# A vision transformer layer on one core: q and k transposed without gap columns and spread by DMA, token tables joined in DRAM, order of work remade

## The reference

```
h = patches @ W_lin.T + b_lin                 # 64 x 196 x 192
h = [cls_tok, cls_token, h]                   # 198 tokens an image
q, k, v = split(layernorm(h) @ w_qkv.T)       # 12 heads of 16
q, k = rope(q * 0.25), rope(k)                # rotation by the token's place
h = h + softmax(q @ k.T) @ v @ w_proj.T + b_proj
h = h + ffn(layernorm(h))
```

## Time and profile before

| | us |
|---|---|
| median of three executions | 1359.68 |
| the profiled execution | 1361.1 |
| its span | 1359.3 |
| TensorE busy (share) | 1312.5 (97%) |
| VectorE | 981.5 (72%) |
| ACT | 901.0 (66%) |
| POOL | 890.1 (65%) |
| mean granted clock of TensorE | 0.974 |

### The profile page before, as it was taken

How to read it: one execution, slowest core, us unless ns; L and a number is a source line. 1 busy time by engine, 2 the same in 40 slices (tenths; PEclk the granted TensorE clock), 3 DMA queues, 4 the chain that set the end, 5 groups by cost and what they waited for, 6 DMA issues and landing times.

```text
span 1359.3 us, 38194 instructions
## 1 busy us (share of the span) xinstructions
PE 1312.5 (97%) x13142; PEld 989.3 (73%) x13142; DVE 981.5 (72%) x2318; ACT 901.0 (66%) x1629; POOL 890.1 (65%) x1610
## 2 busy tenths in 40 slices
PE   6689999999999999999999999999999999999888
PEld 5467777777777777777777777777777777777667
DVE  1346777877777787777787777787777778776665
ACT  1235677677777777777767767767777777776564
POOL 5445676776667777677676676677666777766243
PEclk9779999999999999999999999999999999999799
DMA  5412212222212222222212222222221222200000
GB/s 151 108 39 58 57 45 55 73 67 62 64 48 76 57 68 58 62 57 55 75 56 54 63 66 59 53 72 67 63 62 48 75 57 68 55 24 20 4 20 27
DMA packets 141809, 79.64 MB, mean 59 GB/s; under 512 B 52631, under 2 KB 140918, under 8 KB 141526
## 3 DMA queue, kind: packets, MB, share of 16 engines
q1 hardware_dynamic: 140428, 74.42, 21.1%
q10 hardware_dynamic: 1194, 2.79, 0.8%
HBM read 56.48 MB, written 9.73 MB: 49 GB/s over the span
## 4 chain that ended last, share of the span: by engine, by line
PE 92%; SPq 2%; DVE 2%; ACT 1%; issue 1%; DMA 1%; POOL 1%; POOLq 0%; ACTq 0%; DVEq 0%
PE turn L463 15%; PE score L525 12%; PE turn L481 11%; PE turn L547 10%; PE turn L592 7%; PE score L504 5%; PE turn L534 5%; PE turn L491 4%; PE turn L600 4%; PE turn L573 4%; PE turn L556 3%; PE turn L574 2%; PE turn L610 2%; PE turn L445 2%; PE turn L581 2%; PE turn L566 2%
## 5 line engine op out<-in xcount | busy, mean ns | idle before, releaser
L885 DVE TENSOR_REDUCE nmax<-score 99x8 f32<-99x1584 f32 x192 | 347.0, 1808 | 130.7 <-PE score L504 130.7
L704 ACT ACTIVATE prob<-score 99x1584 f32<-99x1584 f32 x192 | 286.5, 1492 | 88.1 <-PE score L525 88.1
L463 PE MATMUL turn<-wlin,xp 128*128 128x192 f32 x1188 | 228.1, 343 | 7.0 <-DMA xp<-in_x 7.0
L463 PEld LDWEIGHTS turn<-wlin,xp 128*128 128x128 f32 x1188 | 198.5, 196 | 18.5 <-POOL onT L1009 5.1
L1034 POOL TENSOR_TENSOR ropec<-qk,rope 128x384 f32<-128x384 f32 x99 | 99.0, 1000 | 161.0 <-ACT qk L680 161.0
L525 PE MATMUL score<-qkT 17*99 17x198 f32 x3072 | 182.1, 352 | 18.3 <-DMA qkT<-nmaxT 11.0
L525 PEld LDWEIGHTS score<-qkT 17*99 17x99 f32 x3072 | 117.8, 163 | 76.6 <-issue 65.2
L481 PE MATMUL turn<-wqkv,xT 96*128 96x384 f32 x396 | 156.2, 518 | 1.9 <-ACT xT L673 1.8
L547 PE MATMUL turn<-prob,vaug 99*32 99x198 f32 x3072 | 151.9, 337 | 0.0
L1064 POOL TENSOR_TENSOR yg<-y,gout 128x512 f32<-128x512 f32 x99 | 125.6, 1268 | 29.8 <-ACT yr L765 18.4
L934 DVE SCALAR_TENSOR_TENSOR ag<-th,turn 128x512 f32<-128x512 f32 x99 | 68.0, 687 | 75.9 <-ACT th L744 75.9
(11 more groups left out here) (97 smaller groups left out, 2663.3 us busy)
## 6 DMA issues: line engine op xcount, KB each, us to landing
xp<-in_x SPq DMA_DIRECT2D x63, 588.0 KB, 4.7
out<-h SPq DMA_DIRECT2D x99, 96.0 KB, 1.9
qkT<-nmaxT SPq DMA_DIRECT2D x192, 3.1 KB
vaug<-vt SPq DMA_DIRECT2D x30, 78.9 KB
bias<-in_added SPq DMA_DIRECT2D x30, 74.2 KB
win<-in_win ACTq DMA_DIRECT2D x1, 768.0 KB
xp<-in_x SPq DMA_DIRECT2D x2, 294.0 KB, 5.4
wlin<-in_wlin ACTq DMA_DIRECT2D x2, 288.0 KB, 4.1
```

Of the source, the lines that this page charges most:

```text
L463: last = pe.matmul(turn[:, k, 0:D], xp[:, c, place:place + TILE], wlin[:, c, :], start=(c == 0), stop=(c == KC - 1))
L704: act.activation(prob[:, :, 4 * g:4 * g + 4, :].rearrange("p t r n -> p r t n"), score[0:TT, :, 0:2 * TOKENS].rearrange("p r (t n) -> p r ...
L885: dve.tensor_reduce(nmax[:, b % 2, :, 4 * g:4 * g + 4].rearrange("p t r -> p r t"), score[0:TT, :, 0:2 * TOKENS].rearrange("p r (t n) -> p ...
```

## The change

It has three parts.

1. *q and k.* `qkp` has no gaps, so `transpose_qk` makes three transposes of 128 columns instead of six and takes one bank. A column of a transposed chunk is then 128 head dimensions, eight heads. ACT copies them to a new buffer `qkd`, and SyncE (`place_qk`) puts them to every second row of `qkT` with two DMAs a tile (four where the ring wraps). The heads' rows between were set once, 0 for q and 1 for k, by VectorE. The maxima go to row 31 of each head; the score matmuls take 32 rows, those for the maxima 31. `round_qkT` waits for the DMAs instead of ACT.
2. *Tables.* ACT issues six DMAs at the start which join the three tables, twice one after the other, in a scratch array in DRAM; from tile 1 on, one DMA of 128 rows x 224 columns loads a tile's tables, six tiles deep. Tile 0 comes from the three arrays by six DMAs.
3. *Order.* Attention of an image starts two steps later than before (max scores at half step 2 x tile + 10 instead of + 6), `PROJ_AT` with it; there are 118 steps, and the store comes a step earlier after the projection. Each engine's loop body lists the stages in another order.

```diff
-            top.append(max(top[-1] + 1 if top else 0, 2 * (final_tile(b) + 2) + 2))
-        turn.append(top[-1])
+            top.append(max(top[-1] + 1 if top else 0, 2 * (final_tile(b) + 3) + 4))
+        turn.append(top[-1] + 1)
         for g in range(GROUPS):
-            soft.append(max(soft[-1] + 1 if soft else 0, turn[-1] + 2))
-        out.append(soft[-1] + 2)
+            soft.append(max(soft[-1] + 1 if soft else 0, turn[-1] + 1))
+        out.append(soft[-1] + 3)
...
-        steps.append(max(steps[-1] + 1 if steps else 0, (OUT_AT[final_image(i)] + 2) // 2))
+        steps.append(max(steps[-1] + 1 if steps else 0, (OUT_AT[final_image(i)] + 1) // 2))
...
-STEPS = PROJ_AT[-1] + 9
+STEPS = PROJ_AT[-1] + 8
...
+    tab_d = nc.dram_tensor("joined", (2 * TOKENS, TAB), F32, kind="Internal").ap()
...
-        qkp = sb("qkp", [128, 2, 2 * HEADS, 2 * DH])
+        qkp = sb("qkp", [128, 2, QK])
+        qkd = sb("qkd", [128, 2, GROUPS, TILE])
...
+            def load_tab(i):
+                if i >= TABS:
+                    sp.wait_ge(rope_done, i - TABS + 1)
+                at = TILE * i % TOKENS
+                sp.dma_start(tab[:, i % TABS, :], tab_d[at:at + TILE, :]).then_inc(tab_loaded[i % TABS], 16)
...
+            def place_qk(i):
+                if i == 0:
+                    sp.wait_ge(qkT_cleared, 2)
+                sp.wait_ge(qkT_copied, i + 1)
+                over = (TILE * (i + 1) - 1 - QRING) // TOKENS
+                if over >= 0:
+                    sp.wait_ge(st_ready, 3 * over + 3)
+                for place, lo, n in pieces(TILE * i, TILE, QRING):
+                    for half in range(2):
+                        sp.dma_start(qkT[0:128:2, half:2 * GROUPS:2, place:place + n],
+                                     qkd[64 * half:64 * half + 64, i % 2, :, lo:lo + n]).then_inc(qk_placed[i % 2], 16)
...
+            load_tab_parts(0)
             load(1)
-            load_bias(0)
+            sp.wait_ge(tables_joined, 16 * 6)
+            for i in range(1, FIRST_TABS):
+                load_tab(i)
             load(2)
...
-            for s in range(-3, STEPS):
-                for i in tile_at(s + 1):
-                    next_rope(i)
+            for s in range(-2, STEPS):
+                for i in tile_at(s - 6):
+                    place_v(i)
                 for b in at(NMAX_AT, 2 * s):
                     place_max(b)
-                for i in tile_at(s - 2):
-                    place_v(i)
+                for i in tile_at(s - 4):
+                    place_qk(i)
+                for i in at(PROJ_AT, s - 7):
+                    store(i)
+                for i in tile_at(s + 2):
+                    prepare(i)
                 for b in at(NMAX_AT, 2 * s + 1):
                     place_max(b)
...
-                k = take(("qkT", i), 2, qkT_copied, Q_COPIES[i])
-                for side in range(2):
-                    for g in range(GROUPS):
-                        head = side * HEADS + 4 * g
-                        last = pe.transpose(turn[:, k + side, g * TILE:(g + 1) * TILE],
-                                            qkp[:, i % 2, head:head + 4, :].rearrange("p h d -> p (h d)"),
-                                            ident[:, :])
+                k = take(("qkT", i), 1, qkT_copied, i + 1)
+                for c in range(GROUPS):
+                    last = pe.transpose(turn[:, k, c * TILE:(c + 1) * TILE], qkp[:, i % 2, c * 128:(c + 1) * 128],
+                                        ident[:, :])
...
-                        rows = slice(32 * r, 32 * r + DH)
+                        rows = slice(32 * r, 32 * r + 31)
...
-                        rows = slice(32 * r, 32 * r + DH + 1)
+                        rows = slice(32 * r, 32 * r + 32)
...
+            for copy in range(2):
+                rows = tab_d[copy * TOKENS:(copy + 1) * TOKENS, :].rearrange("(h a) c -> a h c", h=2)
+                act.dma_start(rows[:, :, 0:D], bias_d[:, :, :]).then_inc(tables_joined, 16)
+                act.dma_start(rows[:, :, D:D + DH], cos_d[:, :, D:D + DH]).then_inc(tables_joined, 16)
+                act.dma_start(rows[:, :, D + DH:TAB], sin_d[:, :, D:D + DH]).then_inc(tables_joined, 16)
...
             def round_qkT(i):
-                pool.wait_ge(qkT_copied, Q_COPIES[i])
+                pool.wait_ge(qk_placed[i % 2], qk_count(i))
```

More of the change, by code:

```diff
@@ L111, in token_runs, with qk_count @@
     return runs
+def qk_count(i):
+    return sum(32 * len(pieces(TILE * n, TILE, QRING)) for n in range(i % 2, i + 1, 2))
 def beyond(i):
@@ L243, in build @@
         begun_embed = sem("begun_embed")
-        bias_loaded = [sem(f"bias_loaded{p}") for p in range(BBUF)]
-        rope_loaded = [sem(f"rope_loaded{p}") for p in range(TBUF)]
+        tables_joined = sem("tables_joined")
+        tab_loaded = [sem(f"tab_loaded{p}") for p in range(TABS)]
         stored = [sem(f"stored{p}") for p in range(TBUF)]
@@ L258, in build @@
         rope_done = sem("rope_done")
+        qkT_cleared = sem("qkT_cleared")
         qkT_ready = sem("qkT_ready")
         qkT_copied = sem("qkT_copied")
+        qk_placed = [sem(f"qk_placed{p}") for p in range(2)]
         qkT_rounded = sem("qkT_rounded")
@@ L344, in prepare @@
                         load(b + XSLOT)
[L346 to L351, removed]
-                            .then_inc(rope_loaded[i % TBUF], 16)
             def place_v(i):
@@ L620, in _ @@
                     max_scores(n)
+                for b in at(NMAX_AT, 2 * s):
+                    transpose_max(b)
+                for b in at(OUT_AT, 2 * s - 1):
+                    transpose_on(b)
+                for b in at(OUT_AT, 2 * s - 2):
+                    transpose_on(b)
                 for i in tile_at(s):
@@ L683, in copy_qkT @@
                 act.wait_ge(qkT_ready, i + 1)
-                over = (TILE * (i + 1) - 1 - QRING) // TOKENS
-                if over >= 0:
-                    act.wait_ge(st_ready, 3 * over + 3)
-                k = bank_of["qkT", i]
-                src = turn[:, k:k + 2, 0:GROUPS * TILE].rearrange("p a (g n) -> p a g n", g=GROUPS)
-                for place, lo, n in pieces(TILE * i, TILE, QRING):
-                    act.activation(qkT[:, :, place:place + n].rearrange("p (a g) n -> p a g n", a=2),
-                                   src[:, :, :, lo:lo + n], ACT.Copy).then_inc(qkT_copied, 1)
+                if i >= 2:
+                    act.wait_ge(qk_placed[i % 2], qk_count(i - 2))
+                act.activation(qkd[:, i % 2, :, :], turn[:, bank_of["qkT", i], 0:QK].rearrange("p (g n) -> p g n", g=GROUPS),
+                               ACT.Copy).then_inc(qkT_copied, 1)
             def copy_maxT(b):
@@ L961, in _ @@
             dve.memset(ones[:, :], 1.0).then_inc(setup_dve, 1)
-            for s in range(-3, STEPS):
+            dve.memset(qkT[:, 0:GROUPS, :], 0.0).then_inc(qkT_cleared, 1)
+            dve.memset(qkT[:, GROUPS:2 * GROUPS, :], 1.0).then_inc(qkT_cleared, 1)
+            for s in range(-2, STEPS):
                 if s == SUM_STEP:
@@ L1078, in norm_y @@
                 pool.tensor_tensor(kap3[:, c], vpow[:, c], kap[:, c], ALU.mult).then_inc(norm3, 1)
-            for s in range(-3, STEPS):
-                for i in at(PROJ_AT, s - 2):
-                    norm_y(i)
+            for s in range(-2, STEPS):
                 for i in at(PROJ_AT, s):
```

176 lines of the change are left out of this document (78 added, 98 removed).

## The result

The changed kernel takes 1315.21 us (median of four runs, 1313.17 to 1318.29), against 1359.30 us for the kernel before measured beside it: a ratio of 0.968, 95% interval 0.966 to 0.970. The forecast was 1319 us in 1300 to 1348.

| stretch of the span, us | before | predicted | after |
|---|---|---|---|
| start to step 14 | 162.0 (163.4 in the sum) | 125.5 | 127.3 |
| 85 steps, 14 to 98 | 1074.4 | 1044.7 | 1038.6 |
| one of them | 12.64 | 12.29 | 12.22 |
| step 99 to the end | 122.9 | 148.6 | 145.4 |

A forecast was written before the change was run, and what follows sets the result against it. TensorE's own work, 97% busy, was taken to bound the kernel. Start 125.5 + 85 steps x 12.29 (1044.7) + end 148.6 = 1318.8 us of span, plus 0.4: 1319 us, range 1300 to 1348.

The forecast's parts named there:

- The added lag: End of the kernel: two more attention steps at 13.9 us each add 27.8 us.
- A full step: Middle, TensorE: three transposes fewer at 0.109 us each save 0.33 us of 12.62, 28 us over 85 steps.
- sign of a misread transpose: Middle: a step shrinking by other than 0.3 us with TensorE full would mean the transpose's price was misread.
- four borders before and four after: TensorE's changes into score groups: about 0.1 us each, four per step before and after, so left out.
- TensorE stays fed: Middle, score banks: new legs of 2.72 to over 3 us exceed floors of 2.63 and 2.44, the tightest by 0.11.
- Rival 1: Middle: the score loop swallows the saving; legs 0.3 us longer per step lose the 28 us, giving 1347 us; 12%.
- The placing: SyncE's transfers of q and k between ACT's copy and POOL's rounding: 2.3 us to landing after issuing, hidden.
- The start: Up to step 14: 125.5 us against 163.4, with the 11.0 us stall and half the clock's loss gone.
- Step 6: Start: this step begins at 36 to 42 us, taken as 39.5, after six steps of embedding and projections.
- rival 3: Start stays as it is: the stall came from the weights' and x's loads and meets the placings; 1337 us; 12%.
- The eight steps after it: Start, steps 6 to 13: 104.4 us before less 18.3 makes 86 us, bounds 79 to 93.
- The clock: Start: 14.6 us of full clock lost after the stall, half of it (7.3) regained; added score rows cost nothing.

The follow-up runs named there:

- experiment 7: Changed kernel with score matmuls over 17 and 16 rows instead of 32 and 31, leaving out head dimensions and the maximum's row: 1323.80 us.
- 1: Changed kernel with each tile's three transposes of q and k made twice: 1343.86 us.
- 2: Kernel before with only the joined tables and one table load per tile, old order, lag and six transposes: 1349.47 us.
- 9: Kernel before with score matmuls over 32 rows instead of 17 and 16, the added rows of q being zeros: 1346.58 us.
- 3: Changed kernel's q and k transposes, spreading by DMA and joined tables, but in the order and with the lag of the kernel before: 1355.03 us.
- 5: Kernel of 3 with the FFN's output product moved behind the attention's projection, and its addition on VectorE behind the residual: 1336.69 us.
- Experiment 4: Changed kernel with FFN weights loaded in four parts over four steps instead of at once, and summed two steps later: 1306.76 us.
- 6: Kernel of 5 with the FFN weights loaded in four parts over steps 2 to 5: 1333.53 us.
- 10: Changed kernel with 17 rows in the exponential's score matmuls alone, leaving out the maximum's row too: 1323.98 us.
- 11: Changed kernel with 16 rows in the maxima's score matmuls alone: 1315.61 us.

## Why the prediction was right, and where it was not

The time lies 4 us under the forecast, and in part by luck: without the rows' effect on the clock, which the prediction did not know, it would by experiment 7 be some 1324 us, 5 us over. The parts of the change do not add up one by one, since they meet at the start, but three are measured alone: the transposes 28.7 us (1), the tables 8.8 (2), the rows 8.6 to 11.3 (7, 9). The added lag costs its two steps at the end.

- *A full step, 12.29 predicted, 12.22 measured.* Three transposes were priced at 0.33 us, and giving them back costs 0.307. The step before is 12.64 over the 85 steps counted (12.62 was the mean of 87), so it shrank by 0.42 and not by 0.33: the prediction's sign of a misread transpose, without one. The sum held that four borders before and four after cancel. They do in number, but not in size: xr's 0.37 us became 0.22, 0.15 less, and qkp's new border takes only 0.1 back; the embedding gives 0.07. That xr's 0.37 held a wait at the loop's floor besides the border, as the prediction allowed, fits this; no run separates the two.
- *TensorE stays fed.* Right: the score loop has legs of 2.91 and 2.68 us and no wait in the middle. But the argument stood on the new order, and I had not seen how much: with the old one the saving is swallowed (3), by a leg that rows 3 showed at 2.64 us. Rival 1 was given 12% by the margin of the new legs; the row that spoke "against it" (a leg at its floor cost nothing) was really the reason why the saving needed another order. One group moved into that leg recovers 0.30 us a step (5).
- *The placing.* Landing 2.4 us for 2.3, SyncE's two issues 0.66 us each for the allowed 0.5: hidden in the middle, as worked out. The 2.2 us that the Trainium skill ("DMA: Bandwidth & Descriptors", Anatomy of one DMA) gave is a fit for transfers that GpSimd issues; these are SyncE's, and the 2.4 measured decides. That the placing's lateness is what the longer lag is for, the theory of 3, is not borne out: with the old lag TensorE waited 2.1 us in all for the round.
- *The start, 125.5 predicted, 127.3 measured*, came out by two errors of opposite sign. Step 6 was taken at 39.5 us and begins at 44.85, since the weights' load does meet the placings: rival 3 in part, with another victim (POOL's round) and 6.7 us instead of 11. Experiment 4 shows the remedy for this one. The Trainium skill ("DMA: Bandwidth & Descriptors", Why a DMA increments its semaphore by 16 and not by 1) had been held against that rival, because the cuts of the old tables go to few engines; experiment 2 agrees that the tables were at fault (1.6 us instead of 11.0), though not that it was through the number of engines. But that section says nothing of a wide transfer that lands behind 768 KB, and of these the slowest landed 8.4 us after its issue. The eight steps after it then took 127.3 - 44.85 = 82.4 us, for 86.
- *The clock* was the misread term. "More rows take no longer, and I cost the added ones at nothing": the first half holds, the second does not. They hold up the granted clock where TensorE's work has gaps, which is worth 8.6 us in the changed kernel (7) and 11.3 in the one before (9). The loss before was put down to the stall alone, and half of it credited to the stall's end. From 61 to 104 us the clock was 0.66 before, 0.77 with the stall gone and few rows (2), 0.80 in the new order with few rows (7), and 0.88 with all. The end profited too: the whole stretch from step 99 ran at 0.88 and now runs at 0.93, and it is 145.4 us instead of 148.6. With few rows step 14 begins at 130.6 us instead of 127.3, and from tile 98 to the end it takes 163.1 instead of 157.1.

What stays open: which transfer holds up the placing in the old order (5, 6), and why the exponential's rows matter and the maxima's do not (10, 11). Both are eight matmuls a group, the former in float32 (0.86 us), the latter in float32r (0.36 us), and this was not taken apart. How the rows come to move the clock no run shows.

## What to carry to other kernels

A leg that stands at the floor of a loop over another engine hides what is taken out of it: see first which stage can be moved in, then take the work out. Where row-tiled matmuls leave rows of their tile unused, try filling them with zeros: here the time of a matmul did not change, and where TensorE's work had gaps its clock stayed up longer. A large load and the small transfers whose landing an engine's order depends on should not be issued within a few us of each other; split the large one over steps. See in the trace first which load stands ahead of the transfer that is late: splitting the weights took the wait away in 4 and not in 6.

## What was not expected of the hardware

The granted clock followed more than whether TensorE was busy. The changed kernel and the one with few rows have the same starts and the same waits up to 91 us, to 0.1 us, and one goes on at 2.4 GHz, the other at 1.2. In the kernel before, zeros in the added rows were enough to lift the clock of 61 to 104 us from 0.66 to 0.86. The Trainium skill ("TensorE: Matmul & The Clock Gate", Part 1: The HAM clock gate) has the gate go by how busy the engine has been; by that rule experiments 7 and 9 should have changed nothing, and the measurements decide.

Within the middle, at full clock, 17 or 32 rows made no difference to 0.001 us a step in either kernel (12.225 and 12.226, 12.634 and 12.633).
